# Packed gate and value-head weights, and one inversion for two norms, in a fused attention and ternary feed-forward kernel

## The chip, the cores and the metric

The kernel runs on one core of one Trainium2 chip. The metric is device time in microseconds (us), the median of several executions. Engines are named as the profile names them: PE (TensorE, with its weight loads as PEld), DVE (VectorE), ACT (ScalarE), POOL (GpSimd) and SP (SyncE, which only issues transfers here). Each works through its own instructions in order and waits on semaphores.

## The reference, cut to what matters

Input x has 16 batches of 256 tokens and 256 features. There are 16 heads of 128. The scores, the decays and the values go through float32.

```python
x = x + layernorm(attn(layernorm(x)))
x = x + layernorm(ffn(layernorm(x)))

def attn(x):                         # per batch
    q = rope(x @ Wq.T)               # 16 heads x 128
    kp, vp = split(x @ Wkv.T)        # one key and one value, shared by the heads
    g = x @ Wg.T                     # 2 x 16 gates
    h = x @ Wkvh.T                   # 2 x 16 head weights, for keys and values
    log_f = concat([0, log_sigmoid(g)])
    h = cumsum(h * exp(cumsum(log_f)[:-1]))
    k, v = rope(kp * kh), vp * vh    # for each head, by its column of h
    return softmax(mask(q @ k.T / sqrt(128))) @ v @ Wout.T

def ffn(x):                          # ternary weights
    h = silu(x @ Wgate) * (x @ Wup)
    return rms_norm(h) @ Wproj
```

## The kernel before, in words

**Batches and steps.** Attention runs over 16 batches, numbered here 0 to 15, with 8 pairs of heads each, so 128 pairs, and one step for each pair. In `batch(g0, par, steps)` of every engine, `g0` is 8 times the batch's number and `s` the step, 0 to 7. The order of the work on each engine is written out by hand. A pair goes through a pipeline of stages with lags in steps (`LAG`): projection, cosine and swap in step p, rotation (L597 and L607 on POOL) and score (L927, L929 on PE) one step later, softmax (exponents L1229 and L1231 on ACT, inverse sums L1575 on DVE, normalising L631 on POOL) two, turning three, values four and output projection five steps later. L620 on POOL scales the keys for each head. The feed-forward part follows for 16 units and isn't touched.

**Float32 by halves.** Operands of the large projections are split in a high part (rounded to the matmul's type) and a low part. `three_passes` (L769 to L775) multiplies high by high, high by low and low by high. All its matmuls are recorded on L773.

**The front of the next batch.** During a batch the front of the next one is prepared, at the steps in `FRONT`: x is normalised and turned, then in step 1 `project_keys` (L827 to L833) makes the shared key (six passes with `wkv`) and in the other half of the same bank, `F_BANK`, the gates and head weights (six passes with `whg`). `whg` has 64 columns, 32 head weights and 32 gates; the other 64 of its 128 columns are zeros. In step 2 `gates` (ACT, L1185) takes the exponent and `gates_one` (DVE, L1473) adds one. Batch 1's front has its own steps, `FIRST`.

**The norms.** The statistics of x for the batch after the next are taken at `AHEAD`: `stats_x` and `gather_x` (DVE, L1445 and L1450) in steps 3 and 4, and `invert_x` (POOL, L551 to L558) in step 5. The attention's result y of the batch before has its statistics in step 7 and `invert_y` (POOL, L575 to L582) in step 1 (`TAIL`, 9). Each inversion is four small instructions on two columns, one for each tile of 128 tokens: add epsilon, negate the mean, the power -0.5, and the product of both for the bias. ACT's `norm_x` (steps 6 and 7) and `norm_y` (steps 3 and 4) use them.

**The feed-forward weights.** In the background of attention the ternary weights are made in 6 chunks, one in two batches (`WSTEP`). On DVE, `weights_above` (L1622) runs in step 1 and `weights_below` (L1630) in step 2 of batches 2, 4, ... 12, and `weights_sign` (L1646), `weights_change` (L1654) and `weights_finish` (L1661) in steps 0, 1 and 2 of batches 3, 5, ... 13. Within a step, DVE's `weights_below`, `weights_sign` and `weights_finish` come first; the inverse sums, `gates_one`, `stats_x` and `gather_x` follow; then come `weights_above` and `weights_change`, the split of o (L1597), the queries' cosines (L1550), `split_pt` (L1588) and the maxima (L1562 to L1565).

**POOL's order within a step** is L597, L607, L631, L620, then what the tables call for, the inversions first.

Of the kernel before, what the change touches and what calls it, by code (L numbers as in the profile page):

```python
# [21 lines left out]
F32 = mybir.dt.float32  # L22
# [3 lines left out]
ALU = mybir.AluOpType  # L26
# [29 lines left out]
AHEAD = dict(stats_a=3, stats_b=4, invert=5, norm_a=6, norm_b=7)  # L56
# [27 lines left out]
def sandwich_kernel(nc, x, wq, wkv, wkvh, wg, wout, wgu, wproj, rope, out):  # L84
    ctx = ExitStack()
    with ctx:
        def sb(name, shape, dt=F32):
            return ctx.enter_context(nc.sbuf_tensor(name, shape, dt))
# [19 lines left out]
        minus_half = sb("minus_half", [P, NT])  # L108
# [21 lines left out]
        def carve(*shape):  # L130
# [81 lines left out]
        ln1_agg = small[:, 60:64].rearrange("p (t a) -> p t a", a=2)  # L212
        ln1_rstd = small[:, 64:66]
        ln2_stat = small[:, 66:78].rearrange("p (t a) -> p t a", a=6)
        ln2_agg = small[:, 78:82].rearrange("p (t a) -> p t a", a=2)
        ln2_rstd = small[:, 82:84]
        gate_mark = small[:, 84:86]
        ln1_minus, ln2_minus = small[:, 90:92], small[:, 92:94]
        ln1_bias, ln2_bias = small[:, 86:88], small[:, 88:90]
# [36 lines left out]
            sem(k) for k in ("kg_ready", "k_swapped", "k_cos_done", "k_sin_done", "k_ready"))  # L256
        gate_exp, gate_one, decay_done, coef_done, kvw_done, cum_done = (
# [54 lines left out]
        def front_at(g0, s, stage):  # L312

            if g0 == 0 and FIRST.get(stage) == s:
                return PAIRS
            if g0 + 2 * PAIRS < STEPS and AHEAD.get(stage) == s:
                return g0 + 2 * PAIRS
            if 0 < g0 and g0 + PAIRS < STEPS and FRONT.get(stage) == s:
                return g0 + PAIRS

        def tail_at(g0, s, stage):

            if g0 == STEPS and TAIL_LAST[stage] == s:
                return g0 - PAIRS
            back = TAIL[stage] // PAIRS
            if TAIL[stage] % PAIRS == s and g0 >= (back + 1) * PAIRS and (g0 < STEPS or back):
                return g0 - (back + 1) * PAIRS

# [203 lines left out]
        def _(pool):  # L532
# [39 lines left out]
            def invert_y(c0):  # L572
# [5 lines left out]
                pool.wait_ge(ln2_eps, c0 + PAIRS)  # L578
                nc.gpsimd.tensor_tensor(ln2_rstd, ln2_rstd, minus_half[:, 0:NT], ALU.pow).then_inc(ln2_inv, PAIRS)  # L579
                pool.wait_ge(ln2_inv, c0 + PAIRS)  # L580
                pool.wait_ge(ln2_neg, c0 + PAIRS)
# [139 lines left out]
            def batch(g0, par, steps):  # L721
                for s in range(steps):
# [10 lines left out]
                    if not is_first(g0, s) and not is_first(g0, s - 2) and not is_first(g0, s - 3):  # L733
                        normalise(g0, s)
                        scale_keys(g0, par, s)
                    c0 = front_at(g0, s, "invert")
                    if c0 is not None:
                        invert_x(c0)
                    c0 = tail_at(g0, s, "invert")
                    if c0 is not None:  # L740
                        invert_y(c0)
# [26 lines left out]
        def _(pe):  # L768
# [58 lines left out]
            def project_keys(c0, par):  # L827
# [4 lines left out]
                three_passes(F_BANK[:, N:2 * N], [(whg_hi[:, k, :], whg_lo[:, k, :], *xs[k]) for k in range(ET)])\  # L832
                    .then_inc(kg_ready, PAIRS)  # L833

            def first_keys():

                halves = ((F_BANK[:, 0:N], wkv_hi, wkv_lo, slice(0, D)), (F_BANK[:, N:2 * N], whg_hi, whg_lo, slice(0, P)))
# [308 lines left out]
        def _(act):  # L1146
# [16 lines left out]
            def norm_y(c0, tiles):  # L1163

                act.wait_ge(ln2_biased, c0 + PAIRS)
# [16 lines left out]

            def gates(c0):
                act.wait_ge(kg_ready, c0 + PAIRS)
# [170 lines left out]
            def batch(g0, par, steps):  # L1355
                for s in range(steps):

                    exponent(g0, s)
# [62 lines left out]
        def _(dve):  # L1421
# [40 lines left out]
            def keys_cos(c0):  # L1462
# [4 lines left out]
                nc.vector.tensor_tensor(k_cos, F_BANK[:, 0:N], cosk, ALU.mult).then_inc(k_cos_done, PAIRS)  # L1467

# [308 lines left out]
            def batch(g0, par, steps):  # L1777
                if isinstance(g0, int) and g0 == 0:
                    dve.wait_ge(x_second, 16)
                for s in range(steps):  # L1780

                    weights_sum(g0, s)
# [132 lines left out]
```

## Time and profile before

| | us |
|---|---|
| median of 3 runs | 1044.86 |
| lowest to highest | 1044.78 to 1045.16 |
| the profiled execution's own time | 1044.8 |
| its span, first to last instruction | 1043.0 |

The profile shows one execution. It has each engine's busy time, the span in 40 slices, DMA queues, the chain of work that ended last, and groups of instructions by line. The trace behind it can be asked for instructions in order of time, for one line's instructions, and for stretches. Matmuls are pipelined, so the durations of neighbours overlap; the distance of two starts tells what a pass costs.

### The profile page before, as it was taken

What the parts mean: (1) busy time and instruction counts of PE and PEld (TensorE: products, weight loads), DVE (VectorE), ACT (ScalarE), POOL (GpSimd) and SP (SyncE); (2) the same over time, 40 slices, a digit from 0 to 9 for tenths busy, and PEclk for the clock granted to TensorE, in tenths of its full rate; (3) what the DMA queues carried; (4) which work ended last, traced back from release to release, by engine and by line L of the source; (5) the groups of instructions that cost most, each with busy time, mean ns of one, the idle gap of its engine ahead of it and who ended that gap; (6) DMA issues with size and microseconds to landing.
All of it is one profiled execution on the core that took longest, in us unless ns stands there. A gap on an engine that the chain in (4) does not pass through costs nothing.

```text
span 1043.0 us, 25125 instructions
## 1 busy us (share of the span) xinstructions
PE 1025.7 (98%) x7859; PEld 985.8 (95%) x7859; DVE 824.8 (79%) x2824; ACT 868.6 (83%) x2399; POOL 937.8 (90%) x927
## 2 busy tenths in 40 slices
PE   7999999999999999999999999999999999999996
PEld 6899999999999999999999999999999899999996
DVE  6868798878887888888788888887777756766665
ACT  5978898989898889898988898888878777777774
POOL 4889999999999999999999999999999758888776
PEclk9999999999999999999999999999999999999999
DMA  7551111112111111221121112111131000000001
GB/s 262 186 183 42 41 63 41 43 52 72 42 32 62 62 42 33 65 66 44 38 76 43 42 52 62 50 34 63 31 113 31 2 1 12 30 24 22 21 22 41
DMA packets 35124, 58.56 MB, mean 56 GB/s; under 512 B 3136, under 2 KB 16000, under 8 KB 34688
## 3 DMA queue, kind: packets, MB, share of 16 engines
q1 hardware_dynamic: 34992, 56.96, 17.1%
q8 instruction: 63, 1.03, 0.4%
q14 instruction: 69, 0.57, 0.2%
HBM read 50.92 MB, written 9.18 MB: 58 GB/s over the span
## 4 chain that ended last, share of the span: by engine, by line
POOL 57%; PE 21%; issue 14%; DVE 1%; ACT 1%; POOLq 0%; ACTq 0%; DVEq 0%
POOL arena L597 15%; POOL arena L620 13%; POOL arena L631 13%; POOL arena L607 12%; PE psum L1015 12%; PE psum L1053 6%; PE psum L773 2%; POOL arena L579 1%; POOL arena L555 1%; POOL X L588 1%; PE psum L1028 1%; PE psum L1037 0%; POOL arena L563 0%; DVE pt_split L1588 0%; POOL wo_lo L648 0%
## 5 line engine op out<-in xcount | busy, mean ns | idle before, releaser
L631 POOL TENSOR_TENSOR arena<-arena 128x768 f32<-128x768 f32 x128 | 196.3, 1533 | 9.6 <-DVE arena L1575 9.0
L607 POOL TENSOR_TENSOR arena<-arena 128x512 f32<-128x512 f32 x128 | 174.6, 1364 | 10.0
L1588 DVE SCALAR_TENSOR_TENSOR pt_split<-psum,vh_col,pt_split 128x256 fp32r<-128x256 f32 (+1 forms) x512 | 177.0, 407 | 2.9 <-ACT pt_split L1248 2.7
L597 POOL TENSOR_TENSOR arena<-arena,tables 128x512 f32<-128x512 f32 x128 | 165.5, 1293 | 15.2 <-ACT arena L1218 14.4
L620 POOL TENSOR_TENSOR arena<-arena 128x512 f32<-128x512 f32 x127 | 163.0, 1284 | 0.0
L927 PE MATMUL psum<-arena 128*128 128x256 f32 x512 | 154.0, 382 | 3.8 <-POOL arena L607 2.5
L1229 ACT ACTIVATE arena<-arena 128x256 f32<-128x256 f32 x256 | 128.6, 502 | 28.4 <-DVE arena L1565 22.3
L773 PE MATMUL psum<-wo_hi,o_hi 128*128 128x256 f32 x512 | 152.0, 297 | 0.0
L773 PE MATMUL psum<-xt_lo,wq_hi 128*128 128x256 f32 x512 | 144.5, 282 | 0.0
L773 PE MATMUL psum<-xt_hi,wq_lo 128*128 128x256 f32 x512 | 144.4, 282 | 0.0
L773 PE MATMUL psum<-wo_hi,o_lo 128*128 128x256 f32 x512 | 144.2, 282 | 0.0
L773 PE MATMUL psum<-xt_hi,wq_hi 128*128 128x256 f32 x512 | 144.0, 281 | 0.0
L773 PE MATMUL psum<-wo_lo,o_hi 128*128 128x256 f32 x512 | 143.6, 281 | 0.0
L773 PE MATMUL psum<-pt_split,vals_hi 128*128 128x512 f32 (+1 forms) x512 | 142.3, 359 | 0.2
L1015 PE MATMUL psum<-xt_hi,wq_hi 128*128 128x256 f32 x512 | 125.6, 282 | 0.0
L1015 PE MATMUL psum<-xt_lo,wq_hi 128*128 128x256 f32 x512 | 124.4, 284 | 0.0
L1247 ACT ACTIVATE pt_split<-psum,vh_col 128x256 fp32r<-128x256 f32 x256 | 120.7, 472 | 0.1
L1217 ACT ACTIVATE arena<-psum 64x512 f32<-64x512 f32 x128 | 76.1, 595 | 46.6 <-DVE arena L1550 45.3
L1597 DVE TENSOR_TENSOR o_lo<-psum,o_hi 128x512 fp32r<-128x512 f32 x128 | 87.4, 682 | 33.9 <-ACT o_hi L1257 32.8
L929 PEld LDWEIGHTS psum<-arena 128*128 128x128 f32 x512 | 97.2, 190 | 13.3
L1563 DVE CUSTOM_DVE_ANT_0 arena<-psum,mask 128x256 f32<-128x256 f32 x256 | 107.0, 418 | 0.0
L1231 ACT ACTIVATE arena<-arena 128x128 f32<-128x128 f32 x256 | 99.4, 388 | 0.0
(193 smaller groups left out, 3415.8 us busy)
## 6 DMA issues: line engine op xcount, KB each, us to landing
arena<-kh_rows SPq DMA_DIRECT2D x127, 256.0 KB, 3.3
out<-spare SPq DMA_DIRECT2D x15, 256.0 KB, 2.2
arena<-w_rows SPq DMA_DIRECT2D x6, 512.0 KB, 4.7
X<-L_attn_Wout SPq DMA_DIRECT2D x1, 2048.0 KB, 14.5
X<-L_attn_x SPq DMA_DIRECT2D x1, 2048.0 KB, 12.3
arena<-L_attn_Wq SPq DMA_DIRECT2D x1, 1536.0 KB, 10.3
X<-L_attn_x SPq DMA_DIRECT2D x1, 1536.0 KB, 9.5
w_rows<-L_ffn_w_gate_up SPq DMA_DIRECT2D x3, 512.0 KB, 7.7
```

The source lines that it names most:

```text
L597: nc.gpsimd.tensor_tensor(swap, swap, spread, ALU.mult).then_inc(q_sined, 1)
L607: nc.gpsimd.tensor_tensor(q_rot[p % 2], q_cos[p % 2], q_swap[p % 2], ALU.add).then_inc(q_roped, 1)
L620: nc.gpsimd.tensor_tensor(k_head[p % 2], keys[par].unsqueeze(1).to_broadcast([P, HP, N]), kh_all[p % 4], ALU.mult).then_inc(k_scaled, 1)
L631: nc.gpsimd.tensor_tensor(tb, tb, r.unsqueeze(3).to_broadcast([P, HP, 3, P]), ALU.mult).then_inc(p_ready, 1)
L773: last = nc.tensor.matmul(o, a, b, start=start and i == 0, stop=stop and i == len(passes) - 1, skip_group_check=skip)
L927: nc.tensor.matmul(sj[:, 0:2 * P], q[:, j, P:N], kt[:, j, :], start=True, stop=True, skip_group_check=True)
L1015: last = nc.tensor.matmul(bank[c % 2 * 2 + half][:, j * N:(j + 1) * N], wgu_t[:, k, col:col + P], part[:, k, :], start=n == 0 and j == 0, ...
L1229: nc.scalar.activation(tb[:, j, 0:2 * P], tb[:, j, 0:2 * P], ACT.Exp, scale=-1.0, bias=nmax[p % 4][:, 2 * j:2 * j + 1], accum_out=rsum[p % ...
L1231: nc.scalar.activation(tb[:, j, 2 * P:3 * P], tb[:, j, 2 * P:3 * P], ACT.Exp, scale=-1.0, bias=nmax[p % 4][:, 2 * j + 1:2 * j + 2], accum_ ...
L1247: nc.scalar.activation(pt_hi[p % 2][:, j * N:(j + 1) * N], b[:, 0:N], ACT.Copy, scale=vh[:, 0, h:h + 1])
L1563: nc.vector.tensor_tensor_reduce(tb[:, j, 0:2 * P], S_BANK[j][:, 0:2 * P], mask[:, :], -1.0, -MASKED, ALU.add, ALU.min, nmax[p % 4][:, 2 * ...
L1588: last = nc.vector.scalar_tensor_tensor(pt_lo[p % 2][:, o], b[:, i], vh[:, t, h:h + 1], pt_hi[p % 2][:, o].bitcast(F32), ALU.mult, ALU.sub ...
```

## The change

Two things are changed.

The two inversions are made together. From batch 1 on, the statistics of x are taken in step 0 (both tiles, and both aggregations) and inverted in step 1. Where an inversion of y falls in the same step (batches 2 to 13), `invert_both` does both with four instructions on four columns. The small tiles are laid side by side for this. In batch 1 `invert_x` runs alone in step 1; in batches 14 and 15 and at the end `invert_y` runs alone.

The weights for gates and head weights are packed. After the front of batch 1 has used them, `pack_gates` copies the low parts of `whg`'s 64 columns into the unused 64 columns of `whg_hi`, so one stationary tile holds both. Each front from batch 2's on multiplies it by the high and the low part of x: four passes instead of six. The upper 64 partitions of the result belong to the low weights: `move_low` (ACT) copies them out of PSUM, and `add_low` (DVE) adds them to the lower 64. `move_low` stands ahead of the exponents in step 2, `add_low` ahead of everything else of DVE in step 2; the gates' exponent waits for `add_low`. The product of low by low comes in as well, which the three passes left out. The packing alone happens once, in step 7 of batch 0. The first fronts now use 64 columns of `whg` instead of 128.

```diff
-AHEAD = dict(stats_a=3, stats_b=4, invert=5, norm_a=6, norm_b=7)
+AHEAD = dict(stats_a=0, stats_b=0, invert=1, norm_a=6, norm_b=7)
+AHEAD_FIRST = dict(stats_a=3, stats_b=4, invert=5, norm_a=6, norm_b=7)
+Y_ALONE = STEPS - 4 * PAIRS
...
-            if g0 + 2 * PAIRS < STEPS and AHEAD.get(stage) == s:
+            if g0 + 2 * PAIRS < STEPS and (AHEAD if g0 else AHEAD_FIRST).get(stage) == s:
...
+            def invert_both(c0, y0):
+
+                pool.wait_ge(ln1_aggr, c0 + PAIRS)
+                pool.wait_ge(ln2_aggr, y0 + PAIRS)
+                at_least(pool, ln1_done, c0)
+                at_least(pool, ln2_done, y0 + PAIRS)
+                nc.gpsimd.tensor_tensor(ln_rstd, ln_agg[:, :, 1], eps[:, 0:1].to_broadcast([P, 2 * NT]), ALU.add)\
+                    .then_inc(ln1_eps, PAIRS)
+                nc.gpsimd.tensor_tensor(ln_minus, ln_agg[:, :, 0], minus_one[:, 0:1].to_broadcast([P, 2 * NT]), ALU.mult)\
+                    .then_inc(ln1_neg, PAIRS)
+                pool.wait_ge(ln1_eps, c0 + PAIRS)
+                nc.gpsimd.tensor_tensor(ln_rstd, ln_rstd, minus_half[:, :], ALU.pow).then_inc(ln1_inv, PAIRS)
+                pool.wait_ge(ln1_inv, c0 + PAIRS)
+                pool.wait_ge(ln1_neg, c0 + PAIRS)
+                nc.gpsimd.tensor_tensor(ln_bias, ln_minus, ln_rstd, ALU.mult).then_inc(ln1_biased, PAIRS)
...
-                three_passes(F_BANK[:, N:2 * N], [(whg_hi[:, k, :], whg_lo[:, k, :], *xs[k]) for k in range(ET)])\
-                    .then_inc(kg_ready, PAIRS)
+                if c0 == PAIRS:
+                    three_passes(F_BANK[0:4 * H, N:2 * N], [(whg_hi[:, k, 0:4 * H], whg_lo[:, k, 0:4 * H], *xs[k])
+                                                            for k in range(ET)]).then_inc(kg_ready, PAIRS)
+                else:
+                    pe.wait_ge(hg_packed, 1)
+                    for k in range(ET):
+                        for part in xs[k]:
+                            last = nc.tensor.matmul(F_BANK[:, N:2 * N], whg_hi[:, k, :], part,
+                                                    start=k == 0 and part is xs[0][0],
+                                                    stop=k == ET - 1 and part is xs[k][1])
+                    last.then_inc(kg_ready, PAIRS)
...
+            def move_low(c0):
+
+                act.wait_ge(kg_ready, c0 + PAIRS)
+                at_least(act, cum_done, c0)
+                nc.scalar.activation(gate_e[0:4 * H, :], F_BANK[4 * H:P, N:2 * N], ACT.Copy).then_inc(hg_moved, PAIRS)
+
             def gates(c0):
-                act.wait_ge(kg_ready, c0 + PAIRS)
+                if c0 <= PAIRS:
+                    act.wait_ge(kg_ready, c0 + PAIRS)
+                else:
+                    act.wait_ge(hg_added, c0 - PAIRS)
...
+            def pack_gates():
+
+                dve.wait_ge(kg_ready, 2 * PAIRS)
+                nc.vector.tensor_copy(whg_hi[:, :, 4 * H:P], whg_lo[:, :, 0:4 * H].bitcast(F32)).then_inc(hg_packed, 1)
+
+            def add_low(c0):
+
+                dve.wait_ge(hg_moved, c0 - PAIRS)
+                nc.vector.tensor_tensor(F_BANK[0:4 * H, N:2 * N], F_BANK[0:4 * H, N:2 * N], gate_e[0:4 * H, :], ALU.add)\
+                    .then_inc(hg_added, PAIRS)
```

## Rows read from the trace of the kernel before

**Rows 1.** The page, busy us (share of the span) xinstructions of each engine
```profile
PE 1025.7 (98%) x7859; PEld 985.8 (95%) x7859; DVE 824.8 (79%) x2824; ACT 868.6 (83%) x2399; POOL 937.8 (90%) x927
```

**Rows 2.** A stretch of attention: its us, busy us by engine, PEclk, DMA share, GB/s
```profile
440.00:500.00 60.00, 60.00 (x450) 57.35 (x449) 53.04 (x195) 52.55 (x157) 58.06 (x52) 1.00 0.17 50
```

**Rows 3.** PE in order of time, batch 8 step 1: start, us, engine, line, what
```profile
429.19 0.28 PE L773 MATMUL psum<-xt_hi,whg_lo 128*128 128x256 f32 x1
429.31 0.28 PE L773 MATMUL psum<-wo_hi,o_hi 128*128 128x256 f32 x1
```

**Rows 4.** Instructions that use tile whg_hi: duration ns min/median/max, first and last start
```profile
L773 PE MATMUL psum<-xt_hi,whg_hi x30: 278/280/286, 35.2 to 732.9; 128*128 128x256 f32 x30
```

**Rows 5.** PE at three scores: batch 8 step 2, batch 9 steps 0 and 2
```profile
433.87 0.41 PE L927 MATMUL psum<-arena 128*128 128x256 f32 x1
...
470.41 0.28 PE L773 MATMUL psum<-xt_hi,wq_lo 128*128 128x256 f32 x1
470.67 0.48 PE L927 MATMUL psum<-arena 128*128 128x256 f32 x1
...
484.45 0.38 PE L927 MATMUL psum<-arena 128*128 128x256 f32 x1
```

**Rows 6.** POOL in order of time, batch 8, steps 1 and 2
```profile
422.55 1.29 POOL L597 TENSOR_TENSOR arena<-arena,tables 128x512 f32<-128x512 f32 x1
...
425.29 2.35 POOL L631 TENSOR_TENSOR arena<-arena 128x768 f32<-128x768 f32 x1
...
429.18 0.71 POOL L579 TENSOR_TENSOR arena<-arena,minus_half 128x2 f32<-128x2 f32 x1
430.03 1.10 POOL L582 TENSOR_TENSOR arena<-arena 128x2 f32<-128x2 f32 x1
431.09 1.29 POOL L597 TENSOR_TENSOR arena<-arena,tables 128x512 f32<-128x512 f32 x1
432.46 1.29 POOL L607 TENSOR_TENSOR arena<-arena 128x512 f32<-128x512 f32 x1
```

**Rows 7.** POOL in order of time, batch 9, steps 0, 1 and 2
```profile
468.46 2.16 POOL L607 TENSOR_TENSOR arena<-arena 128x512 f32<-128x512 f32 x1
...
480.16 0.20 POOL L582 TENSOR_TENSOR arena<-arena 128x2 f32<-128x2 f32 x1
...
481.68 1.62 POOL L607 TENSOR_TENSOR arena<-arena 128x512 f32<-128x512 f32 x1
```

**Rows 8.** DVE in order of time, batch 8; brackets: idle before, releaser
```profile
419.80 0.69 DVE L1597 TENSOR_TENSOR o_lo<-psum,o_hi 128x512 fp32r<-128x512 f32 x1 [0.28 <-ACT o_hi L1257]
...
425.13 1.19 DVE L1622 TENSOR_TENSOR arena<-arena 128x1024 bf16<-128x1024 bf16 x1
...
429.86 1.22 DVE L1630 TENSOR_TENSOR arena<-arena 128x1024 bf16<-128x1024 bf16 x1
...
431.81 0.41 DVE L1473 TENSOR_SCALAR arena<-psum 32x256 f32<-32x256 f32 x1 [0.23 <-ACT psum L1185]
433.26 0.69 DVE L1597 TENSOR_TENSOR o_lo<-psum,o_hi 128x512 fp32r<-128x512 f32 x1 [1.04 <-ACT o_hi L1257]
```

**Rows 9.** ACT in order of time, batch 8, steps 0 to 2
```profile
421.79 0.59 ACT L1218 ACTIVATE arena<-psum 64x512 f32<-64x512 f32 x1
...
429.48 0.51 ACT L1229 ACTIVATE arena<-arena 128x256 f32<-128x256 f32 x1 [0.73 <-DVE arena L1565]
...
432.63 0.60 ACT L1257 ACTIVATE o_hi<-psum 128x512 fp32r<-128x512 f32 x1 [0.91 <-PE psum L773]
```

**Rows 10.** Single lines over the whole run: duration ns min/median/max, first and last start
```profile
L1445 DVE BATCH_NORM_STATS2 arena<-X x32: 374/376/428, 3.7 to 697.8; 128x6 f32<-128x256 f32 x32
...
L1450 DVE BATCH_NORM_AGGREGATE arena<-arena x32: 147/166/183, 4.6 to 698.4; 128x2 f32<-128x6 f32 x32
...
L1180 ACT ACTIVATE arena<-psum x16: 380/382/382, 11.6 to 739.9; 64x256 f32<-64x256 f32 x16
...
L1661 DVE TENSOR_TENSOR arena<-arena x6: 685/1780/1826, 176.4 to 683.0; 128x1024 bf16<-128x1024 bf16 x6
```

More of the change, by code:

```diff
@@ L211, in sandwich_kernel @@
         ln1_stat = small[:, 48:60].rearrange("p (t a) -> p t a", a=6)
[L212 to L216, printed above, removed]
+        ln2_stat = small[:, 60:72].rearrange("p (t a) -> p t a", a=6)
+        ln_agg = small[:, 72:80].rearrange("p (t a) -> p t a", a=2)
+        ln_rstd, ln_bias, ln_minus = small[:, 80:84], small[:, 86:90], small[:, 90:94]
+        ln1_agg, ln2_agg = ln_agg[:, 0:NT, :], ln_agg[:, NT:2 * NT, :]
+        ln1_rstd, ln2_rstd = ln_rstd[:, 0:NT], ln_rstd[:, NT:2 * NT]
+        ln1_bias, ln2_bias = ln_bias[:, 0:NT], ln_bias[:, NT:2 * NT]
+        ln1_minus, ln2_minus = ln_minus[:, 0:NT], ln_minus[:, NT:2 * NT]
         gate_mark = small[:, 84:86]
-        ln1_minus, ln2_minus = small[:, 90:92], small[:, 92:94]
-        ln1_bias, ln2_bias = small[:, 86:88], small[:, 88:90]
         x2_stat = small3[:, 0:12].rearrange("p (t a) -> p t a", a=6)
@@ L327, in tail_at, with both_at @@
                 return g0 - (back + 1) * PAIRS
+        def both_at(g0, s):
+            c0, y0 = front_at(g0, s, "invert"), tail_at(g0, s, "invert")
+            if c0 is not None and y0 is not None:
+                return c0, y0
         def head_count(g, j):
@@ L735, in batch @@
                         scale_keys(g0, par, s)
+                    both = both_at(g0, s)
                     c0 = front_at(g0, s, "invert")
-                    if c0 is not None:
+                    if both:
+                        invert_both(*both)
+                    elif c0 is not None:
                         invert_x(c0)
                     c0 = tail_at(g0, s, "invert")
-                    if c0 is not None:
+                    if c0 is not None and not both:
                         invert_y(c0)
@@ L1356, in batch @@
                 for s in range(steps):
+                    c0 = front_at(g0, s, "gates")
+                    if c0 is not None and c0 > PAIRS:
+                        move_low(c0)
                     exponent(g0, s)
@@ L1780, in batch @@
                 for s in range(steps):
+                    c0 = front_at(g0, s, "gates_one")
+                    if c0 is not None and c0 > PAIRS:
+                        add_low(c0)
+                    if is_first(g0, s - 7):
+                        pack_gates()
                     weights_sum(g0, s)
```

16 lines of the change are left out of this document (10 added, 6 removed).

## The prediction

> **What bounds the kernel now.** I read the page first. TensorE (PE) is busy for 98% of the span [rows 1], and in a stretch of the attention part for 60.00 of 60.00 us at a granted clock of 1.00; GpSimd (POOL) is busy for 58.06 of 60 there [rows 2]. So two engines are nearly full, and the question for each edit is which of them ends last at the place it touches. I number batches 0 to 15 and steps 0 to 7 (a step is one pair of heads, pair p is projected in step p and scored in step p+1). The timeline of PE gives the unit: one 128x256 pass of the projections follows the other every 0.12 us [rows 3].
>
> The place where PE and POOL meet is the score (L927), which needs the rotated queries of L607. Three meetings matter. (1) Step 2 of batch 8: L607 ends at 432.46+1.29 = 433.75, the score starts at 433.87 [rows 5, 6], on PE's beat, so PE loses nothing, but it has no slack either. This repeats in batches 2, 4, ... 12 (call them even), six times. (2) Step 2 of batch 9: L607 ends at 481.68+1.62 = 483.30, the score is at 484.45 [rows 5, 7]: 1.1 us of slack, the same in batches 3, 5, ... 13 (odd). (3) Step 0 of batch 9, for the last pair of batch 8: L607 takes 2.16 instead of 1.29 us [rows 7], and the score comes 0.26 us behind the last pass (470.41 to 470.67) and its first matmul takes 0.48 instead of 0.41 or 0.38 [rows 5]: about 0.25 us lost, again six times. Elsewhere I find PE at its 0.12 us beat.
>
> Why (1) is tight: in even batches VectorE (DVE) runs two weight steps beside POOL. From 425.13 on (L1622, 1.19 us) POOL's L631 takes 2.35 us, and from 429.86 on (L1630, 1.22 us) POOL's last small instruction L582 takes 1.10 us [rows 6, 8], where the same instruction takes 0.20 in batch 9 [rows 7]. POOL stood still for some 0.9 us each time. The Trainium skill (SBUF — State Buffer, section "SBUF: two separate sides") says that a DVE instruction with two SBUF inputs and a GpSimd instruction exclude each other for a whole instruction; the trace agrees, with these two.
>
> **The change part by part.**
>
> *Packed gates (PE).* Six passes on whg become four in every batch's front from the third batch's on. The 30 passes by xt_hi and whg_hi [rows 4] are two for each of 15 fronts; the first of these (batch 1's, made during batch 0) stays at six, so 14 fronts lose two passes each: 14 x 2 x 0.12 = 3.4 us of PE work, between the scores of step 1 and step 2. Where PE sets the end of that step, it is gained in full (0.24 us each); where POOL is at zero slack (place 1), nothing of it is gained.
>
> *The addition it needs.* ACT moves 64x256 out of PSUM ahead of the exponents of step 2, 0.38 us by the nearest row, L1180 [rows 10]. ACT waited 0.73 us there for DVE's maxima, and 0.91 us later in the same step for PE [rows 9]; the last whg pass ends at 429.19+0.28 = 429.47 [rows 3], 0.24 us earlier after the change, and the exponents start at 429.48. So I cost it at zero; without that cover it is 0.38 us in step 2. DVE adds 64x256 in PSUM ahead of L1630; the row nearest in kind (L1473) takes 0.41 us [rows 8], I estimate 0.35 from start to start, since neighbours overlap by some 0.06. Behind it stand L1630 or L1661, the inverse sums, gates_one and the split of o, which waited 1.04 us for ACT in that step [rows 8]; it costs nothing by itself, but moves L1630 0.35 us later against POOL. The gates' exponent then waits for the sum, which is done long before ACT's last exponent. The single packing copy is one instruction in the first batch: 0 to 0.4 us once, taken as 0.
>
> *Inversions together (POOL).* Of 8 small instructions in a batch 4 remain, in 12 batches (2 to 13). A set without the stall takes 1.3 us: three plain ones of 0.20 and a power of 0.70 [rows 6, 7]. They vanish from step 5, where PE does not wait. What is late next there is the loss at place 3: POOL arrives earlier by up to 1.3 us, but L597 of that step must wait for the swapped queries and can start only about 0.24 us earlier; that still covers nearly all of the 0.25 us. Gain 6 x 0.25 = 1.5 us.
> The joint power works on 4 columns. No row shows one. Bounds: 0.70 us, if the columns' number does not matter (a power of 2 columns takes 0.70, a plain instruction 0.20), and 0.70+0.50 = 1.20 us, if all above the plain one grows with the columns. I take 0.70, the row of the same operation, and keep 1.20 for the range.
>
> *Statistics moved (DVE).* For batches from 3 on, both bn_stats and both bn_aggr stand in step 0 instead of steps 3 and 4: 2x0.376 + 2x0.166 = 1.08 us [rows 10], some 0.9 with the overlap of neighbours. In step 0 they stand ahead of the split of o (L1597), which waited only 0.28 us for ACT [rows 8]. So the rest of DVE's step comes 0.6 us later: cosines, then ACT's swap (L1218, ending at 422.38 [rows 9]), then POOL's L597, which starts at 422.55 [rows 6], right behind it. In even batches POOL therefore starts step 1 about 0.6 us later. ACT's exponents, L1575 and L1622 move with it, so L631 ends 0.6 us later too. In odd batches POOL is later than the swap by itself, and I count 0.5 us at L1654 and L631.
>
> *Sum at place 1, even.* In the trace's times: L582 without its stall would end at 430.2, so the joint set ends at 430.2+0.6 = 430.8 (a power of 0.70, no stall inside), and L1630 wants to begin at 429.86+0.6+0.35 = 430.8: a tie. If L597 comes first, it runs, L1630 waits and then holds L607 back by 0.87, as at place 3 [rows 7]; L607 ends at 430.8+1.37+2.16 = 434.3, 0.55 later than before. If L1630 comes first, L597 starts at 432.0, L607 ends at 434.65: 0.85 or so later. The saved 0.24 us of PE is swallowed. With place 3, an even batch changes by +0.3 to +0.6 us; six: +1.8 to +3.6.
> *Odd.* L607 ends 0.5 us later, at 483.8; PE wants it at 484.45-0.24 = 484.2 [rows 5]: still no wait, so -0.24 each: -1.4 us. *The two fronts in batches 1 and 14* give -0.5 us.
> Total: -0.1 to +1.7, middle +0.7. The profiled execution (span 1043.0, time 1044.8) becomes 1045.5; the median 1044.86 is the same within 0.1 us. That is about no change.
>
> **The rivals.**
> (A) Slower: the power grows with the columns. The page GPSIMD Engine Reference of the Trainium skill ("Performance versus the Vector engine") has GpSimd loop over the elements of a partition, with 2.6 cycles for each, which speaks for it; by the trace it is the 0.50 us above a plain instruction that would double. Place: the joint set in step 1. Price: at even batches L1630 always comes first and L607 ends at about 434.7 (+0.9, less 0.25); at odd ones the set ends at 481.3, L1661 (0.69 alone, up to 1.83 beside POOL [rows 10]) may come first and costs PE 0 to 0.6 us against before. Six of each and -0.5: +3.5 to +7, most likely +4, 1048.8. It decides from a power of about 0.8 us on in even batches, from 1.1 on in odd ones.
> (B) Faster: DVE's statistics find cover, or POOL's earlier finish of step 0 lets its chain run ahead, so that L607 is never late. Then all of 3.4 us and the 1.5 us of place 3 come in: 1040.0. For it: POOL gets 1.3 us a batch back. Against it: L597 in step 1 waits for the swap, which the statistics make later.
> (C) It does not do what it says: the passes saved turn into waiting on PE everywhere, because the added chain PE, ACT, DVE, ACT or the order of the steps holds the exponents back, and the gain of PE is zero in odd batches too: the sum without -1.9, +2.6, 1047.4. Against it speak the idle times of 0.73 and 0.91 us on ACT.
>
> **How the numbers follow.** Forecast (power 0.70, tie at place 1) 50%, 1045.5, its own range 1043.5 to 1047. Rival A 22%, B 16%, C 7%, and 5% for something worse. Low end 1039.5, so that B is mostly in; high end 1050.0, which leaves out the end of A. A measurement of this kernel can tell about 0.2% (2.1 us) from no change. Faster by more than that: B and a little of the forecast, 0.20. Slower: A, half of C, the rest, and the upper tail of the forecast, 0.32. Same: 0.48.
>
> **What would show it right or wrong.** PE: whg passes 0.12 us apart, four of them, 14 times. Step 2 of even batches: a gap ahead of the score of 0.5 to 0.9 us, released by the line that L607 becomes, and the odd ones without a gap. Step 0 of odd batches: a score without the 0.26 us. POOL: duration of the power on 4 columns (0.70 or 1.20). DVE: split of o in step 0 about 0.6 us later after the statistics, and L597 of step 1 of even batches later by as much against PE's beat. If these L597 start where they did, the forecast is wrong and B right; if the power takes 1.2 us, A; if odd batches show a gap too, A or C, told apart by which of POOL and ACT was late.

## The result, and the profile after

The changed kernel took 1046.97 us (median of 17 runs, 1046.56 to 1048.66), the kernel before 1044.93 beside it (17 runs). The ratio is 1.0018, 95% interval 1.0012 to 1.0025: 2 us longer, just inside the 0.2% that count as no change, though the interval reaches past it. Of nine runs of the kernel e10 below one took 5446.02 us; it is in that kernel's median and not in its ratio. The profiled execution of the changed kernel took 1047.22 with a span of 1045.1, so its span grew by 2.1 us against the one of before.

The page of the kernel after (busy us, share of the span, instructions; then two groups with busy us, mean ns | idle before, and what ended it):

```profile
PE 1023.1 (98%) x7831; PEld 982.8 (94%) x7831; DVE 817.5 (78%) x2839; ACT 873.7 (84%) x2413; POOL 929.8 (89%) x879
...
L622 POOL TENSOR_TENSOR arena<-arena,tables 128x512 f32<-128x512 f32 x128 | 164.8, 1288 | 22.5 <-ACT arena L1267 21.8
...
L964 PE MATMUL psum<-arena 128*128 128x256 f32 x512 | 153.9, 382 | 8.6 <-POOL arena L632 7.3
```

Against [rows 1] PE has 28 matmuls less (14 fronts of two) and 2.6 us less to do, and POOL 48 instructions and 8.0 us less. Yet PE finished later: it now stands still for 7.3 us ahead of the scores (L964, before L927), waiting for the rotated queries (L632, before L607). The same group of before has 2.5 us there. The other lines that moved: L597 is now L622, L631 is L656, L620 is L645, and L579 and L582 have their joint twins in L580 and L583; on DVE L1630 is L1693, L1622 is L1685, L1597 is L1660, and the new addition is L1529; on ACT L1218 is L1267, L1229 is L1278, and the new move is L1227.

POOL of the kernel after in order of time, batch 8, steps 1 and 2, to be laid beside [rows 6] (start, us, engine, line, what, in brackets idle before):

```profile
423.26 1.28 POOL L622 TENSOR_TENSOR arena<-arena,tables 128x512 f32<-128x512 f32 x1 [0.39 <-ACT arena L1267]
...
430.00 1.03 POOL L580 TENSOR_TENSOR arena<-arena,minus_half 128x4 f32<-128x4 f32 x1
431.16 1.10 POOL L583 TENSOR_TENSOR arena<-arena 128x4 f32<-128x4 f32 x1
432.22 1.29 POOL L622 TENSOR_TENSOR arena<-arena,tables 128x512 f32<-128x512 f32 x1
433.58 1.27 POOL L632 TENSOR_TENSOR arena<-arena 128x512 f32<-128x512 f32 x1
```

The chain starts 0.71 us later (423.26 against 422.55). Of this 0.29 is in PE's score of step 1 too (its first matmul at 426.86; 426.57 before), so against PE it is 0.42 later. The power on four columns takes 1.03 us. What stands in POOL's way behind it is on DVE (same kernel, batch 8, steps 0 and 2):

```profile
419.73 0.70 DVE L1497 BATCH_NORM_STATS2 arena<-X 128x6 f32<-128x256 f32 x2
420.53 0.25 DVE L1502 BATCH_NORM_AGGREGATE arena<-arena 128x2 f32<-128x6 f32 x2
420.70 0.66 DVE L1660 TENSOR_TENSOR o_lo<-psum,o_hi 128x512 fp32r<-128x512 f32 x1
...
430.66 0.42 DVE L1529 TENSOR_TENSOR psum<-psum,arena 64x256 f32<-64x256 f32 x1
430.99 1.21 DVE L1693 TENSOR_TENSOR arena<-arena 128x1024 bf16<-128x1024 bf16 x1
```

L1693 starts at 430.99, before L583, which takes 1.10 us in place of 0.20. So L632 ends at 434.85, against 433.75 before: 0.81 later against PE. On PE of the kernel after, score of batch 8 (step 2) and of batch 9 (step 2):

```profile
433.80 0.28 PE L801 MATMUL psum<-xt_hi,wq_lo 128*128 128x256 f32 x1
434.91 0.70 PE L964 MATMUL psum<-arena 128*128 128x256 f32 x2 [0.84 <-POOL arena L632]
...
484.87 0.28 PE L801 MATMUL psum<-xt_hi,wq_lo 128*128 128x256 f32 x1
484.99 0.62 PE L964 MATMUL psum<-arena 128*128 128x256 f32 x2
```

Even batches have a gap of 0.84 (batch 2: 0.65), odd ones none. Odd ones had nothing to spare either: there DVE's `weights_finish` (L1724, before L1661) holds L583, which takes 0.73 us in place of 0.20 [rows 7]:

```profile
481.51 0.73 POOL L583 TENSOR_TENSOR arena<-arena 128x4 f32<-128x4 f32 x1
...
481.51 0.67 DVE L1724 TENSOR_TENSOR arena<-arena 128x1024 bf16<-128x1024 bf16 x1
```

Distances of score starts give the account, here and in all that follows counted at the first weight load of each score, which starts about 0.1 us ahead of the first matmul where PE does not wait. From step 1 to step 2: even 7.34 before, 8.16 after (batch 2: 7.97); odd 7.29 to 7.33 before, 7.08 after; batches 1 and 14 7.30 and 7.05. The last pair's score in step 0 of the next batch (place 3): 6.15 before, 5.89 after. In all, an even batch became 0.52 longer, an odd one 0.25 shorter, and from the first score to the last attention takes 802.89 us before and 803.80 after: +0.9. The other 1.2 us of the span lie behind the last score, nearly all of it at the end of the feed-forward part, whose code is the same (last section).

### The profile page after: what moved, and what is told of

It is laid out like the page before. It is cut to its first block, busy times and chain, and to the rows that moved or that the text cites. A ratio compares the mean times of both kernels' runs of the same rounds, so it can differ in the third digit from the quotient of the medians.

```text
span 1045.1 us, 25054 instructions
## 1 busy us (share of the span) xinstructions
PE 1023.1 (98%) x7831; PEld 982.8 (94%) x7831; DVE 817.5 (78%) x2839; ACT 873.7 (84%) x2413; POOL 929.8 (89%) x879
## 3 DMA queue, kind: packets, MB, share of 16 engines
q8 instruction: 63, 1.03, 0.4%
## 4 chain that ended last, share of the span: by engine, by line
POOL 56%; PE 21%; issue 16%; DVE 1%; ACT 1%; POOLq 0%; ACTq 0%; DVEq 0%
POOL arena L622 14%; POOL arena L645 14%; POOL arena L656 12%; POOL arena L632 12%; PE psum L1052 12%; PE psum L1090 6%; PE psum L801 2%; POOL arena L580 1%; PE psum L1065 1%; PE psum L1074 1%; POOL arena L588 0%; POOL X L613 0%; DVE pt_split L1651 0%; POOLq L304 0%; POOL wo_lo L673 0%
## 5 line engine op out<-in xcount | busy, mean ns | idle before, releaser
L656 POOL TENSOR_TENSOR arena<-arena 128x768 f32<-128x768 f32 x128 | 195.6, 1528 | 13.6 <-DVE arena L1638 13.4
L622 POOL TENSOR_TENSOR arena<-arena,tables 128x512 f32<-128x512 f32 x128 | 164.8, 1288 | 22.5 <-ACT arena L1267 21.8
L632 POOL TENSOR_TENSOR arena<-arena 128x512 f32<-128x512 f32 x128 | 172.9, 1351 | 10.0
L645 POOL TENSOR_TENSOR arena<-arena 128x512 f32<-128x512 f32 x127 | 162.9, 1283 | 0.0
L964 PE MATMUL psum<-arena 128*128 128x256 f32 x512 | 153.9, 382 | 8.6 <-POOL arena L632 7.3
L1278 ACT ACTIVATE arena<-arena 128x256 f32<-128x256 f32 x256 | 128.5, 502 | 20.5 <-DVE arena L1628 13.6
L1660 DVE TENSOR_TENSOR o_lo<-psum,o_hi 128x512 fp32r<-128x512 f32 x128 | 87.3, 682 | 35.2 <-ACT o_hi L1306 34.5
```

The lines of the kernel that those rows point to most:

```text
L622: nc.gpsimd.tensor_tensor(swap, swap, spread, ALU.mult).then_inc(q_sined, 1)
L632: nc.gpsimd.tensor_tensor(q_rot[p % 2], q_cos[p % 2], q_swap[p % 2], ALU.add).then_inc(q_roped, 1)
L645: nc.gpsimd.tensor_tensor(k_head[p % 2], keys[par].unsqueeze(1).to_broadcast([P, HP, N]), kh_all[p % 4], ALU.mult).then_inc(k_scaled, 1)
L656: nc.gpsimd.tensor_tensor(tb, tb, r.unsqueeze(3).to_broadcast([P, HP, 3, P]), ALU.mult).then_inc(p_ready, 1)
L964: nc.tensor.matmul(sj[:, 0:2 * P], q[:, j, P:N], kt[:, j, :], start=True, stop=True, skip_group_check=True)
L1278: nc.scalar.activation(tb[:, j, 0:2 * P], tb[:, j, 0:2 * P], ACT.Exp, scale=-1.0, bias=nmax[p % 4][:, 2 * j:2 * j + 1], accum_out=rsum[p % ...
```

## The experiments

Every kernel was timed beside the kernel before. "Attention" is the distance from the first score to the last, in the profiled execution; the last two columns are the distances from the score of step 1 to that of step 2. The profiled executions of e4, e10 and e11 took 1.3, 1.4 and 1.9 us longer than the medians of these kernels, in e4 and e11 with a first score 1 us later than in the kernel before; so medians are to be compared with medians, and attention with attention.

| label | median, before beside it (us) | ratio, 95% | attention | even | odd |
|---|---|---|---|---|---|
| before | | | 802.89 | 7.34 | 7.31 |
| after | 1046.97, 1044.93 | 1.0018, 1.0012 to 1.0025 | 803.80 | 8.16 (batch 2: 7.97) | 7.08 |
| e1_pack_only | 1045.17, 1044.75 | 1.0004, 0.9995 to 1.0013 | 803.00 | 7.66 to 7.79 | 7.05 to 7.09 |
| e2_joint_only | 1046.38, 1044.75 | 1.0016, 1.0007 to 1.0025 | 803.82 | 7.85 (batch 2: 7.67) | 7.30 |
| e3_stats_early | 1044.09, 1044.75 | 0.9995, 0.9986 to 1.0004 | 800.97 | 7.67 | 7.08 |
| e4_below_late | 1046.48, 1044.75 | 1.0016, 1.0007 to 1.0025 | 803.45 | 7.29 (batch 2: 7.08) | 7.08 |
| e5_joint_step2 | 1043.33, 1045.18 | 0.9987, 0.9978 to 0.9996 | 800.45 | 7.05 | 7.05 to 7.09 |
| e6_joint_step2_stats0 | 1047.13, 1045.18 | 1.0013, 1.0004 to 1.0022 | 804.77 | 7.05 | 7.07 |
| e7_before_y_step2 | 1047.47, 1045.18 | 1.0020, 1.0010 to 1.0029 | 805.64 | 7.30 | 7.30 to 7.33 |
| e8_pack_y_step2 | 1048.41, 1045.18 | 1.0031, 1.0019 to 1.0043 | 806.02 | 7.05 | 7.05 to 7.09 |
| e11_pack_no_add | 1043.07, 1044.87 | 0.9984, 0.9974 to 0.9993 | 801.07 | 7.35 to 7.38 (batch 12: 7.51) | 7.07 to 7.09 |
| e10_step2_y1_last | 1042.37, 1044.87 | 0.9974, 0.9964 to 0.9984 | 799.81 | 7.05 | 7.05 to 7.09 |

**Packing alone (e1).** The two inversions stay apart, in their old steps.

```diff
-AHEAD = dict(stats_a=0, stats_b=0, invert=1, norm_a=6, norm_b=7)
-Y_ALONE = STEPS - 4 * PAIRS
+AHEAD = dict(stats_a=3, stats_b=4, invert=5, norm_a=6, norm_b=7)
+Y_ALONE = 0
...
-            if c0 is not None and y0 is not None:
-                return c0, y0
+            return None
```

> The packing alone; statistics and inversions stand as in the kernel before. Theory (the loss comes from the statistics in step 0 and the longer power in step 1, not from the packing): the last score, at 822.88 us in the kernel before and 823.78 in the changed one, comes at 820.2 to 822.2; odd batches take 7.08 us from the score of step 1 to that of step 2 instead of 7.33 and keep slack ahead of it, even ones 7.1 to 7.5. Time 0.5 to 3 us under the kernel before. Rival (moving and adding the low half is what costs): the last score comes at 823 or later and the even batches keep 8 us.

Attention did not get shorter at all, a miss; the last score came at 823.00, where the rival had it, though even batches did not keep its 8 us. Odd batches give 0.25, even ones lose 0.32 to 0.45. DVE, POOL and PE of e1 in batch 8 (L1528 is the addition, L1692 the old L1630, L606 the old L582):

```profile
429.83 0.42 DVE L1528 TENSOR_TENSOR psum<-psum,arena 64x256 f32<-64x256 f32 x1
430.17 1.20 DVE L1692 TENSOR_TENSOR arena<-arena 128x1024 bf16<-128x1024 bf16 x1
...
430.00 1.43 POOL L606 TENSOR_TENSOR arena<-arena 128x2 f32<-128x2 f32 x1
...
434.09 0.70 PE L963 MATMUL psum<-arena 128*128 128x256 f32 x2 [0.33 <-POOL arena L631]
```

The addition puts the weight step 0.31 us later than in [rows 8] (430.17 against 429.86). POOL's L606 starts where L582 did and ends with it, so it takes 1.43 in place of 1.10, and L631 comes 0.33 us later.

**The addition left out (e11).** As e1, but nothing adds the low half: gates and head weights then lack their part by the low half of the weights.

```diff
-                if c0 <= PAIRS:
-                    act.wait_ge(kg_ready, c0 + PAIRS)
-                else:
-                    act.wait_ge(hg_added, c0 - PAIRS)
+                act.wait_ge(kg_ready, c0 + PAIRS)
...
-                    if c0 is not None and c0 > PAIRS:
+                    if False:
                         add_low(c0)
```

> The packing alone with inversions apart, and VectorE's addition of the low half left out, so the gates and head weights lack the product of their low half; the time is what is read. Theory: the addition's 0.33 us in front of weights_below is what made even batches 7.66 us long there: L582 is held instead of L597 and L607, they take 7.34, odd ones 7.07, last score at 821.1 (823.0 with the addition). Rival (ACT's move of the low half is what costs): even batches stay at 7.66, last score 823.0.

DVE and POOL of e11 in batch 8 (L1689 is the old L1630):

```profile
429.93 1.22 DVE L1689 TENSOR_TENSOR arena<-arena 128x1024 bf16<-128x1024 bf16 x1
...
430.10 1.10 POOL L606 TENSOR_TENSOR arena<-arena 128x2 f32<-128x2 f32 x1
```

Both are back within 0.07 us of their places in [rows 6, 8], the even distance falls to 7.35 to 7.38 (7.34 before: PE's saving is worth nothing there, since POOL has no slack), and attention is 1.9 us shorter than in e1, as forecast. The last score came at 822.10 and not at 821.1, since the first was 1 us late too. The packing saved its passes in both; ACT's move was in both and cost nothing that shows. What spent the gain is DVE's 0.33 us ahead of a weight step that holds POOL.

**The joint inversion alone (e2).** Six passes, no move, no addition.

```diff
-                    for k in range(ET):
-                        for part in xs[k]:
-                            last = nc.tensor.matmul(F_BANK[:, N:2 * N], whg_hi[:, k, :], part,
...
+                three_passes(F_BANK[:, N:2 * N], [(whg_hi[:, k, :], whg_lo[:, k, :], *xs[k]) for k in range(ET)])\
+                    .then_inc(kg_ready, PAIRS)
```

> Statistics in step 0 and the joint inversion alone; six passes for the gates and no moving and adding. Theory: even batches take about 7.8 us from the score of step 1 to that of step 2 (8.16 in the changed kernel, less the 0.33 us by which the addition moved L1630 later), odd ones stay at 7.3, the place at step 0 gives 0.26 back; last score at about 824.3, time 1 to 3 us over the kernel before. Rival (the packing's chain costs): even batches at 7.34, last score at 821.3, faster than before by 1.5 us.

Forecast 7.8 for even batches, measured 7.85, with L583 at 0.77 us (POOL and PE of e2, batch 8):

```profile
431.28 0.77 POOL L583 TENSOR_TENSOR arena<-arena 128x4 f32<-128x4 f32 x1
...
434.71 0.70 PE L955 MATMUL psum<-arena 128*128 128x256 f32 x2 [0.28 <-POOL arena L632]
```

**Statistics taken one batch earlier, in steps 3 and 4 (e3).** The rest is the changed kernel; the lines stand ahead of the table of fronts, where `s` is the step and `stage` the entry of `AHEAD`.

```diff
+            if stage in ("stats_a", "stats_b") and g0 > 0:
+                if g0 == PAIRS and s == 0:
+                    return g0 + 2 * PAIRS
+                if AHEAD_FIRST[stage] == s and g0 + 3 * PAIRS < STEPS:
+                    return g0 + 3 * PAIRS
+                return None
```

> The changed kernel, but with the statistics of x back in steps 3 and 4, one batch earlier, so that step 0 of VectorE is as before; the joint inversion stays in step 1. Theory: L597 of step 1 starts 0.4 to 0.8 us earlier against PE, even batches take 7.66 us instead of 8.16 (the power of 1.02 us still meets L1630), odd ones 7.08 with slack; last score at about 821.3, time about 1 to 2 us under the kernel before. If the statistics did not matter: 8.16 stays, last score 823.8.

POOL and PE of e3, batch 8 (L628, L589, L638 are L622, L583, L632 of the kernel after):

```profile
421.46 1.30 POOL L628 TENSOR_TENSOR arena<-arena,tables 128x512 f32<-128x512 f32 x1
...
429.29 1.11 POOL L589 TENSOR_TENSOR arena<-arena 128x4 f32<-128x4 f32 x1
...
433.05 0.70 PE L970 MATMUL psum<-arena 128*128 128x256 f32 x2 [0.34 <-POOL arena L638]
```

Even batches need 7.67 (forecast 7.66) in place of 8.16, and attention is 2.8 us shorter than in the changed kernel; the time came out 0.7 us under the kernel before, where I had forecast 1 to 2. So the statistics in step 0 cost 0.5 us in an even batch, although DVE had 0.28 us of idle time to give there [rows 8]. L589 still takes 1.11: the stall itself stays. And e3, with one power on four columns, needs the same in even batches as e1, with a power on two (7.67 and 7.66): the longer power costs nothing there.

**The weight step moved one step on (e4).**

```diff
-WSTEP = dict(cast=5, sum=6, scale=7, above=9, below=10, decide=14, sign=16, change=17, finish=18, turn=23, copy=23,
+WSTEP = dict(cast=5, sum=6, scale=7, above=9, below=11, decide=14, sign=16, change=17, finish=18, turn=23, copy=23,
```

> The changed kernel, but weights_below (1.2 us on VectorE, at the top of step 2 of even batches) one step later. Theory (the shared port with GpSimd decides at step 2): the last small instruction of the joint inversion takes 0.2 instead of 1.1 us, even batches take 7.24 instead of 8.16 us from the score of step 1 to that of step 2, and step 3 gives back 0 to 0.4 us; last score at 820 to 822. Rival (the statistics and the longer power decide by themselves): 8.16 becomes no less than 7.9.

POOL and DVE of e4, batch 8, steps 2 and 3:

```profile
431.98 0.20 POOL L583 TENSOR_TENSOR arena<-arena 128x4 f32<-128x4 f32 x1
...
438.80 2.15 POOL L632 TENSOR_TENSOR arena<-arena 128x512 f32<-128x512 f32 x1
...
437.96 1.84 DVE L1693 TENSOR_TENSOR arena<-arena 128x1024 bf16<-128x1024 bf16 x1
```

The stall is gone from the joint set (0.20) and from the distance (7.29; forecast 7.24), and stands one step later on L632: the next three distances are 6.16, 6.34 and 5.99 where 5.88 is PE's own. They give 0.84 us back; I had expected 0 to 0.4. The last score came at 824.47 for a forecast of 820 to 822. Moving the weight step moves the wait more than it removes it.

**The inversions in step 2 (e5, e6).** In e5 with the early statistics of e3, in e6 with those in step 0.

```diff
-AHEAD = dict(stats_a=0, stats_b=0, invert=1, norm_a=6, norm_b=7)
+AHEAD = dict(stats_a=0, stats_b=0, invert=2, norm_a=6, norm_b=7)
-TAIL = dict(copy=5, stats=7, invert=9, norm_a=11, norm_b=12, add=14)
+TAIL = dict(copy=5, stats=7, invert=10, norm_a=11, norm_b=12, add=14)
```

> The changed kernel with the joint inversion in step 2 instead of 1 (norms of y follow in step 3 as before) and the statistics of x in steps 3 and 4, one batch earlier. Theory: what costs is only that the inversion, the two weight steps of VectorE and the statistics all fall ahead of the score of step 2; GpSimd has room at step 3. Even batches take 7.1 us from the score of step 1 to that of step 2, later steps of the batch give back 0 to 0.2 us, odd ones 7.08; last score at 817 to 819 (823.78 in the changed kernel, 822.88 before), time 4 to 5.5 us under the kernel before. Rival (GpSimd is full over the whole batch, so the wait only moves to steps 3 to 5): last score no earlier than 820.5.

> The changed kernel with the joint inversion in step 2 alone; the statistics of x stay in step 0. Theory: the 0.8 us by which they make L597 of step 1 late are covered up to the score of step 2 (7.1 to 7.3 us in even batches), and cost 0.1 to 0.4 us at the next score; last score at 818 to 820, 1 us behind the kernel with early statistics. If the statistics cost their full 0.6 to 0.8 us in each even batch: last score 822.

POOL and PE of e5 (batch 8; then batch 15):

```profile
428.65 2.31 POOL L638 TENSOR_TENSOR arena<-arena 128x512 f32<-128x512 f32 x1
...
435.08 0.20 POOL L589 TENSOR_TENSOR arena<-arena 128x4 f32<-128x4 f32 x1
...
790.89 0.70 PE L970 MATMUL psum<-arena 128*128 128x256 f32 x2 [1.94 <-POOL arena L638]
```

Both missed. In e5 the last score came at 820.62 for a forecast of 817 to 819, just past the 820.5 before which the rival would not have it, and the time is 1.9 us under the kernel before for 4 to 5.5; in e6 it came at 824.69 for 818 to 820, and 822 in its worse case. The score of step 2 is on PE's beat in both kernels (7.05). Behind it e5 gives some 0.4 us back in each even batch (6.08, 5.99, 5.99 in batch 8, where 5.88 is PE's own), e6 0.9 (6.57, 5.98, 5.99). And in both there is a place that I had not looked at: in batch 15 one distance is 8.09, where the kernel before has 7.03, and in e6 the next is 7.43 for 5.87. POOL of e5 there (L613 ends the inversion of y, L693 the one of the feed-forward's first norm):

```profile
786.26 0.72 POOL L613 TENSOR_TENSOR arena<-arena 128x2 f32<-128x2 f32 x1
...
788.07 0.19 POOL L693 TENSOR_TENSOR arena<-arena 128x2 f32<-128x2 f32 x1
788.22 1.28 POOL L628 TENSOR_TENSOR arena<-arena,tables 128x512 f32<-128x512 f32 x1
```

The feed-forward's own inversion (`invert_x2`) stands in that step already, so two sets follow one another there, ahead of the rotation that the score waits for. Neither of my expectations had priced it.

**Is it the place of the inversion of y (e7, e8)?** The same edit of `TAIL` alone, in the kernel before (e7) and in the kernel of e1, which only packs (e8).

```diff
-TAIL = dict(copy=5, stats=7, invert=9, norm_a=11, norm_b=12, add=14)
+TAIL = dict(copy=5, stats=7, invert=10, norm_a=11, norm_b=12, add=14)
```

> The kernel before with invert_y in step 2 instead of 1, nothing else. Theory: PE did not wait at the score of step 2, so nothing is gained where nothing is made shorter: last score at 822.9 within 0.4, time the same within 0.5 us; slack ahead of that score in even batches grows from 0.05 to over 0.5 us. Rival (the place of the inversion is the whole gain): last score at 820 or earlier.

> The packing alone, with separate inversions, invert_y in step 2, invert_x in step 5. Theory: odd batches 7.07, even ones 7.1 from the score of step 1 to that of step 2 (7.66 with invert_y in step 1), but GpSimd still has both inversions, and in even batches a wait of 0.2 to 0.4 us appears at steps 3 to 6; last score at 820.5 to 821.5. If the joint inversion's relief is not needed: 818.5.

Both came out later than forecast: the last score at 825.43 for 822.9 in e7 (the time 2.3 us over the kernel before, for the same within 0.5), and at 825.91 for 820.5 to 821.5 in e8. In e7 nothing is gained up to batch 14: PE sets the distances anyway (7.30). In e8 the even distance is 7.05, but the wait turns up again at the score of step 6 (7.24 to 7.30, in batch 12 7.15, where 6.58 is free). In both, batch 15 takes two distances too many: 8.37 and 7.50 in e7 for 7.03 and 5.87, 8.07 and 7.43 in e8; that is 3.0 and 2.6 us. PE and the stretches of e7 there (columns as in [rows 2]):

```profile
794.12 1.22 PE L927 MATMUL psum<-arena 128*128 128x256 f32 x2 [2.22 <-POOL arena L607]
```

```profile
790.00:794.00 4.00, 1.90 (x16) 1.70 (x14) 2.90 (x8) 3.84 (x13) 3.78 (x7) 1.00 0.13 45
794.00:798.00 4.00, 3.88 (x16) 3.53 (x17) 1.37 (x11) 2.81 (x8) 3.95 (x4) 0.57 0.05 6
798.00:802.00 4.00, 4.00 (x33) 3.85 (x32) 0.97 (x3) 2.26 (x9) 3.95 (x3) 1.00 0.24 59
```

PE was busy for 1.90 of 4 us, waited 2.22 for POOL, and then had a granted clock of 0.57: nearly all of that stretch at 1.2 GHz, the lower of its two levels. It did 16 matmuls in 4 us where the next stretch has 33. So in this execution one late rotation costs twice: 1.3 us at once (8.37 for 7.03), and 1.6 in the next distance, at the lower clock. Not every execution need pay the second time (last section).

**The inversion of y kept in step 1 at the end (e10).** As e5, but in batches 14 and 15 `invert_y` stays in step 1, apart from the feed-forward's.

```diff
+            at = 9 if stage == "invert" and g0 >= STEPS - 2 * PAIRS else TAIL[stage]
```

> The kernel with the joint inversion in step 2 and early statistics, but where the inversion of y runs alone (batches 14, 15 and the drain) it is back in step 1. Theory: in batch 15 the score-to-score distances that were 5.88 and 8.09 us there return to 5.98 and 7.05, so the last score comes 0.9 us earlier, at 819.7, and the time is 2.5 to 3.5 us under the kernel before. If batch 15 was late for another reason, the last score stays at 820.6.

The group of scores in e10, to be laid beside that of the kernel after:

```profile
L971 PE MATMUL psum<-arena 128*128 128x256 f32 x512 | 155.0, 384 | 3.8 <-POOL arena L639 2.4 <-issue 0.6 <-DVE vals_lo L1583 0.6
```

Waiting for POOL is down from 7.3 to 2.4 us, as in the kernel before, with 28 matmuls less; batch 15 is back at 5.98 and 7.05 as forecast, attention is 3.1 us shorter than before and 4.0 shorter than after, and the time 2.5 us shorter than before. It is the quickest kernel of this study, and computes what the changed one computes.

**What a power costs (e9).** The changed kernel with 18 powers on the mask's tile at its end, two each on 1, 2, 3, 4, 6, 8, 16, 32 and 64 columns of 128 partitions, each waiting for the one before. Its own time, 1095.43 us, says nothing.

```diff
+            for n in (1, 2, 3, 4, 6, 8, 16, 32, 64):
+                for _ in range(2):
+                    pool.wait_ge(powers, done)
+                    nc.gpsimd.tensor_tensor(mask[:, 0:n], mask[:, 0:n], mask[:, P:P + n], ALU.pow).then_inc(powers, 1)
+                    done += 1
```

> The changed kernel, with eighteen powers of 1, 2, 3, 4, 6, 8, 16, 32 and 64 columns (two of each) on GpSimd added behind its last work; its time says nothing. If the power has a fixed part and a part for each column, as 0.70 us for 2 and 1.02 for 4 say, each column takes 0.16 us: 0.54 for 1, 1.65 for 8, 2.9 for 16, 10.5 for 64. If it goes in groups of 4 or of 16 columns, 4 and more columns take steps instead.

The line in e9 (ns min/median/max, first and last start, forms):

```profile
L801 POOL TENSOR_TENSOR mask<-mask x18: 553/1321/10545, 1041.8 to 1082.4; 128x1 f32<-128x1 f32 x2, 128x2 f32<-128x2 f32 x2, 128x3 f32<-128x3 f32 x2, 128x4 f32<-128x4 f32 x2
```

They took 0.55, 0.70, 0.85, 1.01, 1.32, 1.64, 2.90, 5.43 and 10.54 us: close to a straight line of 0.38 us and 0.16 for each column.

## Why the prediction came out as it did

Forecast 1045.5 in a range of 1039.5 to 1050.0, no change the likeliest; measured 1046.97. The range held, and "no change" did by a hair. Attention, which is all that the sum was about, came out at +0.9 for a forecast of +0.7 (-0.1 to +1.7). Another 1.2 us came from where the sum had nothing, so that the time is still inside the forecast's own range, which ended at 1047, is luck.

- **PE's saving: right.** 14 fronts of four passes 0.12 us apart; the odd batches and batches 1 and 14 each gave 0.25 us, as forecast.
- **Odd batches: right by a hair.** The step said, in the times of the kernel before, that L607's twin ends at 483.8 and PE wants it at 484.2. These are 0.81 us later in the kernel after, 484.6 and 485.0. It ended at 484.85, with the score at 484.99: no wait, but 0.14 of slack in place of 0.4. The 0.5 us that I had put on DVE's statistics were not the whole: L583 lost 0.53 to `weights_finish`, a meeting that I had only in rival A.
- **The power on four columns: mis-sized, and it did not matter in even batches.** I took 0.70, the row of the same operation on two, since it seemed a fixed cost. It took 1.02 (the row below), between my two bounds, 0.70 and 1.20. With 0.70, L583 would have started at 430.84, 0.15 us ahead of L1693 at 430.99: the tie stood where the step put it. But e1 shows how such a tie ends: with a power on two columns, L606 started at 430.00, 0.17 us ahead of the weight step, and was held all the same. So by e1 the weight step would have come first at 0.70 too; no run has that very case in the changed kernel, but e3 and e1 take the same time in even batches. The Trainium skill (GPSIMD Engine Reference, "Performance versus the Vector engine") has GpSimd loop over the elements; e9 agrees in form, as each column of a power adds 0.16 us to 0.38.
- **Place 1, even: the later of the two cases, right in size.** "If L1630 comes first": +0.85 on the score, measured 0.82. With place 3 that was +0.6 for an even batch; measured +0.52, within +0.3 to +0.6. L632's end is set by the end of L1693, not by the power.
- **Rival A came half true.** Its condition (a power above 0.8) held, and its even batches happened, though not by the power; its odd ones were to start only from 1.1 us on. At 1.02 the weight step held L583 there already, but took 0.67 itself, and they gained their 0.25. I had bundled both in one case with +4 us as its likeliest.
- **Place 3: right.** 6.15 became 5.89, 0.26 each for a forecast of 0.25.
- **Statistics in step 0: right in kind, a third less on POOL.** I counted 0.6 us for DVE's split and for POOL's start. The split came 0.61 later behind the same predecessor (1.09 us after the start of the reciprocal ahead of it, 0.48 before), POOL's start 0.42 against PE's beat, and e3 prices the whole at 0.5 in each even batch.
- **The addition "costs nothing by itself, but moves L1630 by 0.35": right in size (0.33), too low in weight.** I had not drawn what follows for the packing taken by itself. e1 and e11 show it: 0.3 us in each even batch, 1.9 in all, which is over half of what the packing saves.
- **The move on ACT: right.** It took 0.38 us (below), and 0.28 us of idle time was left behind it.
- **Rival C did not happen:** no exponent was late for the added chain. Rival B did not either; e3 and e10 show that part of its 4.9 us was to be had (1.9 and 3.1 us of attention), but with the statistics, in e10 the inversions too, elsewhere.
- **What I did not see:** 1.2 us outside attention. They brought the span from +0.9 to +2.1; the sum had taken the feed-forward part for unchanged, as its code is.

Line L580 of the kernel after (ns min/median/max), and ACT of it in batch 8:

```profile
L580 POOL TENSOR_TENSOR arena<-arena,minus_half x12: 1017/1022/1030, 125.2 to 683.5; 128x4 f32<-128x4 f32 x12
```

```profile
429.61 0.38 ACT L1227 ACTIVATE arena<-psum 64x256 f32<-64x256 f32 x1
430.27 0.51 ACT L1278 ACTIVATE arena<-arena 128x256 f32<-128x256 f32 x1 [0.28 <-DVE arena L1628]
```

## What to carry to other kernels

Where one engine is full and a second arrives at its meetings without slack, work saved on the first is worth nothing there, and what the edit adds in front of the second, on whatever engine, can cost its full length, as the addition's 0.33 us did: price the helpers (an addition, moved statistics) by what starts later behind them, not by whether their own engine has time. Two instructions merged in one save their fixed cost alone (of two powers 0.38 us here), so find how the operation grows with its size before the merger is called free. Before a step is moved, look at the first and last rounds of the loop too: what stands in the target step only there can cost more than all the others gain.

## What the runs showed of the hardware

**A stall that looks like work.** The same small product took 0.20, 0.77, 1.10 and 1.43 us in e4, e2, the kernel after and e1 (there on two columns), by how much of DVE's weight step of 1.2 us was still to come when it started. It was held to the end of that step even in e1, where it had started 0.17 us ahead of it, while DVE was at the addition: of two starts so close the earlier one does not tell which engine goes on. Whether the addition held it first is not shown.

**PE's clock after a wait.** In e7 a wait of 2.22 us was followed by a stretch at 0.57 of the clock; in e8, with 1.92, the same stretch, 794 to 798, has 0.70, and in e6, with 1.94, it has 0.59. In e5, with a wait of 1.94 us at the same score, it has 1.00. So it isn't the length of the wait that decides. It may differ from one execution of a kernel to the next: of eleven of e7 three have spans of 1044.1 to 1044.5 us at a mean granted clock of 0.997 or 0.998, and eight have 1045.6 to 1047.4 at 0.996, the profiled one (1045.6) among them. Only one execution of each kernel has a trace, so where the others lost their time is not shown.

The end of the kernel after shows something of the kind. The last of PE's waits, and the stretches:

```profile
1036.72 0.51 PE L1090 MATMUL psum<-wq_lo,wo_hi 128*128 128x256 f32 x1 [2.14 <-POOL wo_lo L673]
```

```profile
1034.00:1036.00 2.00, 0.58 (x5) 0.38 (x4) 1.97 (x2) 0.37 (x1) 2.00 (x2) 1.00 0.00 0
1036.00:1038.00 2.00, 1.28 (x6) 1.28 (x7) 0.95 (x1) 0.00 (x0) 1.55 (x2) 0.71 0.39 131
1038.00:1040.00 2.00, 1.38 (x8) 1.29 (x7) 1.05 (x5) 0.00 (x0) 0.40 (x1) 0.50 0.34 114
```

From 1036.82 to PE's end the clock is at 1.2 GHz, and the passes are 0.21 us apart. In the kernel before they came behind a wait of 2.07 us at full clock, 0.12 us apart:

```profile
1035.42 0.39 PE L1053 MATMUL psum<-wq_lo,wo_hi 128*128 128x256 f32 x1 [2.07 <-POOL wo_lo L648]
...
1035.00:1037.00 2.00, 1.56 (x12) 1.48 (x12) 0.97 (x2) 0.00 (x0) 1.55 (x2) 1.00 0.33 113
```

There it fell at 1038.07, with PE's matmuls done. From the end of that wait to the end of the span the kernel before needs 7.6 us and the kernel after 8.4: 0.8 of the 1.2 us. The same happened in e3, e4, e10 and e11, not in e1, e2, e5, e6, e7 and e8. Here too the wait does not decide: e2 had 2.15 us and kept its clock, and e11 had the 2.07 of the kernel before and lost it (its passes are 0.21 us apart behind the line below). What does stays open, and so does how much of these 0.8 us belongs to the changed kernel and how much to the execution that was profiled.

```profile
1034.72 0.58 PE L1089 MATMUL psum<-wq_lo,wo_hi 128*128 128x256 f32 x1 [2.07 <-POOL wo_lo L672]
```

The other 0.4 us stand ahead of that wait, most of it where POOL stands still for 0.43 us in the last unit, in unchanged code, as it does not in the kernel before:

```profile
1031.87 0.20 POOL L700 TENSOR_TENSOR arena<-arena 128x2 f32<-128x2 f32 x1 [0.43 <-POOL arena L697]
```

It shows in e2, e3, e4, e5, e6, e9 and e10 too, in the same place: in every kernel with the joint inversion, and in none without it (before, e1, e7, e8, e11). What joins the two, no run here tells.
